# An attention-and-feed-forward kernel on one core: V products in fewer visits, maxima further ahead, and half of the rotary step on other engines

## The reference: what is computed

```
h = layernorm(x) * (1 + ca) + sa
q, k, v = split(h @ qkv_w.T + qkv_b); q, k = rope(q), rope(k)
attn = softmax(causal_mask(q @ k.T / sqrt(8))); x = x + ga * (attn @ v @ proj_w.T + proj_b)
h = layernorm(x) * (1 + cb) + sb
y = square(relu(h @ W_fc.T)) @ W_proj.T; x = x + gb * mean_of_5_spikes(y)
```

## Time and profile before

| | |
|---|---|
| median of 3 runs | 489.86 us (484.31 to 490.41) |
| the profiled execution | 488.89 us, of it a span of 487.2 us |
| busy: PE, DVE, ACT, POOL | 87%, 65%, 53%, 25% of the span |
| granted clock of PE, mean | 0.916 |

### The profile page before, as it was taken

One profiled execution on the slowest core, in us unless ns is written; L12 is line 12 of the kernel. 1 busy time (PEld: TensorE's weight loads), 2 busy tenths in 40 slices (PEclk: granted clock), 3 DMA queues, 4 the chain that ended last, 5 costly groups with the idle time before them and its releaser, 6 DMA issues.

```text
span 487.2 us, 14412 instructions
## 1 busy us (share of the span) xinstructions
PE 425.2 (87%) x6007; PEld 253.6 (52%) x6007; DVE 317.8 (65%) x719; ACT 256.0 (53%) x445; POOL 123.7 (25%) x159
## 2 busy tenths in 40 slices
PE   3448999889999999999999999999999999988752
PEld 2214564455546565565556654656556656645422
DVE  2768776747873978478865687388837674720735
ACT  1111465456476555755685447656665476666220
POOL 7624020501342141404240323213240310130210
PEclk9865699669999989999999699999999899999958
DMA  6166514141313232233214241323133220010000
GB/s 198 51 170 191 149 40 112 57 122 49 106 51 102 69 108 63 70 100 111 71 56 121 60 101 53 103 63 105 50 96 78 74 81 5 26 30 20 23 0 22
DMA packets 26043, 38.45 MB, mean 79 GB/s; under 512 B 5794, under 2 KB 20714, under 8 KB 23690
## 3 DMA queue, kind: packets, MB, share of 16 engines
q1 hardware_dynamic: 25978, 37.53, 26.8%
HBM read 26.35 MB, written 8.65 MB: 72 GB/s over the span
## 4 chain that ended last, share of the span: by engine, by line
PE 67%; DVE 16%; issue 4%; POOL 4%; ACT 4%; DMA 4%; SPq 1%; POOLq 0%; ACTq 0%; DVEq 0%
PE s_bank L447 15%; PE o_bank L498 12%; PE t_bank L480 10%; PE d_bank L554 6%; PE d_bank L547 5%; DVE negmax L778 4%; PE a_bank L518 4%; PE s_bank L453 3%; PE t_bank L485 2%; DMA den<-o_raw 2%; PE a_bank L525 2%; PE a_bank L467 2%; PE d_bank L537 2%; DVE xn L794 2%; DVE rot_s L814 2%
## 5 line engine op out<-in xcount | busy, mean ns | idle before, releaser
L778 DVE TENSOR_REDUCE negmax<-s_bank 128x1 f32<-128x448 f32 (+7 forms) x368 | 194.3, 566 | 99.9 <-PE s_bank L453 98.5
L664 ACT ACTIVATE probs<-t_bank 128x512 f32<-128x512 f32 x288 | 167.0, 596 | 118.0 <-PE t_bank L485 114.4
L447 PE MATMUL s_bank<-kf,qf 72*64 72x448 bf16 (+7 forms) x1024 | 127.1, 315 | 10.8 <-DVE negmax L778 10.5
L480 PE MATMUL t_bank<-qf,kf 74*64 74x512 bf16 (+7 forms) x1024 | 115.6, 297 | 4.2 <-ACT probs L664 4.1
L447 PEld LDWEIGHTS s_bank<-kf,qf 72*64 72x64 bf16 x1024 | 49.6, 114 | 101.8 <-DVE negmax L778 62.4
L498 PE MATMUL o_bank<-probs,v 128*32 128x512 f32 (+7 forms) x1024 | 92.5, 436 | 0.0
L453 PE MATMUL s_bank<-causal,identb 128*64 128x64 bf16 x1024 | 74.9, 202 | 0.0
L485 PE MATMUL t_bank<-causal_t,identb 128*64 128x64 bf16 x1024 | 65.2, 197 | 0.0
L480 PEld LDWEIGHTS t_bank<-qf,kf 74*64 74x64 bf16 x1024 | 41.4, 114 | 27.7 <-ACT probs L664 10.3
L485 PEld LDWEIGHTS t_bank<-causal_t,identb 128*64 128x64 bf16 x1024 | 49.1, 114 | 10.8
L453 PEld LDWEIGHTS s_bank<-causal,identb 128*64 128x64 bf16 x1024 | 49.4, 117 | 0.2
(11 more groups left out here) (106 smaller groups left out, 386.7 us busy)
## 6 DMA issues: line engine op xcount, KB each, us to landing
qf<-q_scr SPq DMA_DIRECT2D x15, 576.0 KB
kf<-k_scr SPq DMA_DIRECT2D x45, 192.0 KB
q_scr<-parts SPq DMA_DIRECT2D x24, 128.0 KB, 1.7
k_scr<-parts SPq DMA_DIRECT2D x24, 128.0 KB, 1.7
xa<-in_x SPq DMA_DIRECT2D x8, 256.0 KB, 3.5
o_t<-o_raw SPq DMA_DIRECT2D x60, 32.0 KB, 2.0
rden<-r_scr SPq DMA_DIRECT2D x15, 128.0 KB
out_y<-count SPq DMA_DIRECT2D x7, 256.0 KB, 2.3
```

The lines of the kernel that those rows point to most:

```text
L447: nc.tensor.matmul(bank[C * a:C * (a + 1), col:col + keys], qf[0:FR, slot, 2 * p + a, C * i:C * (i + 1)], kf[0:FR, slot, 2 * p + a, 0:keys ...
L480: nc.tensor.matmul(bank[C * a:C * (a + 1), col:col + w], kf[0:KX, slot, 2 * p + a, C * kb:C * (kb + 1)], qf[0:KX, slot, 2 * p + a, C * kb: ...
L664: nc.scalar.activation(probs[:, v, :], t_bank[u % 2][:, :], ACT.Exp, scale=SCALE).then_inc(e_done, 1)
L778: last = nc.vector.tensor_reduce(own[:, i, p:p + len(same)], cols, AX.X, ALU.max, negate=True)
```

## The change

Four things change. (1) The V products of a half run in four visits: key blocks 0, 1 and 7 after slot 9, 2 and 6 after slot 13, 3 and 5 after slot 0 of the next half, and 4 after its slot 1. Before they ran in eight, after slots 5, 9, 10, 13, 14, 17, 0 and 1. (2) `S_LEAD` is 31. (3) From batch 1 on, the two sine instructions of DVE are gone. ACT copies the projection with its bias to the other 64 partitions in two instructions (`swap_halves`, into the one buffer `rot_s[:, 0]`), POOL multiplies by the sines (`sines`, into `rot_s[:, 1]`), and DVE keeps the product with the cosines (`cosines`), which waits for ACT's copies as well. ACT's copies stand ahead of the exponentials of slots at = 25 and 29, DVE's product in slots at = 26 and 30, and POOL's product right ahead of each `rotary_sum`. (4) ACT's casts of the parts move a slot later, to after the exponentials of slots at = 29, 31, 33 and 35. SP's program stays as it is.

```diff
-S_LEAD = 29
+S_LEAD = 31
...
-PV_AFTER = {5: (0,), 9: (1,), 10: (7,), 13: (2,), 14: (6,), 17: (3,)}
-PV_LATE = {0: (5,), 1: (4,)}
+PV_AFTER = {9: (0, 1, 7), 13: (2, 6)}
+PV_LATE = {0: (3, 5), 1: (4,)}
...
-            for kb in (5, 4):
+            for kb in (3, 5, 4):
                 probs_times_v(HALVES - 1, kb)
...
+            def swap_halves(b, qk):
+
+                act.wait_ge(a_ready, 4 * b + QK + qk + 1)
+                reach(act, sines_done, 2 * (b - 1) + qk)
+                act.wait_ge(whole_done, 1)
+                for to, of in ((slice(0, 64), slice(64, P)), (slice(64, P), slice(0, 64))):
+                    nc.scalar.activation(rot_s[to, 0, :], a_bank[of, :], ACT.Identity, bias=bqk_sb[of, qk:qk + 1],
+                                         scale=1.0).then_inc(swapped, 1)
+
...
+            swap_halves(1, 0)
             for j in range(2):
                 take_part(1, 0, j)
+            swap_halves(1, 1)
...
-            TAKE_AT = {-8: (0, 0), -6: (0, 1), -4: (1, 0), -2: (1, 1)}
+            SWAP_AT = {-11: 0, -7: 1}
+            TAKE_AT = {-7: (0, 0), -5: (0, 1), -3: (1, 0), -1: (1, 1)}
...
+                if at - PER_BATCH in SWAP_AT and b + 2 < NB:
+                    swap_halves(b + 2, SWAP_AT[at - PER_BATCH])
...
+            def cosines(b, qk):
+                dve.wait_ge(a_ready, 4 * b + QK + qk + 1)
+                reach(dve, whole_done, 2 * (b - 1) + qk + 1)
+
+                dve.wait_ge(swapped, 2 * (2 * (b - 1) + qk + 1))
+                nc.vector.scalar_tensor_tensor(rot_c[:, qk, :], a_bank[:, :], bqk_sb[:, qk:qk + 1], cos_sb[:, :],
+                                               ALU.add, ALU.mult).then_inc(a_free, 1)
+
...
-            ROTARY_AT = {-11: (0, 0), -10: (0, 1), -9: (0, 2), -7: (1, 0), -6: (1, 1), -5: (1, 2)}
+            COSINES_AT = {-10: 0, -6: 1}
...
+            def sines(b, qk):
+
+                pool.wait_ge(swapped, 2 * (2 * (b - 1) + qk + 1))
+                pool.wait_ge(whole_done, 2 * b + qk)
+                nc.gpsimd.tensor_tensor(rot_s[:, 1, :], rot_s[:, 0, :], sin_sb[:, :], ALU.mult)\
+                    .then_inc(sines_done, 1)
+
...
             for qk in range(2):
+                sines(1, qk)
                 rotary_sum(1, qk)
...
                 if b + 2 < NB:
+                    sines(b + 2, 0)
                     rotary_sum(b + 2, 0)
                     left(b + 2, 0, 1)
                     left(b + 2, 0, 2)
+                    sines(b + 2, 1)
                     rotary_sum(b + 2, 1)
```

More of the change, by code:

```diff
@@ L245, in adaln_kernel @@
         rotated = sem("rotated")
+        swapped = sem("swapped")
+        sines_done = sem("sines_done")
         whole_done = sem("whole_done")
@@ L813, in rotary @@
                                       (slice(64, P), slice(0, 64), rot_s, sin_sb))[step]
-                nc.vector.scalar_tensor_tensor(dst[to, qk, :], bank[of, :], bqk_sb[of, qk:qk + 1], table[of, :],
+                nc.vector.scalar_tensor_tensor(dst[to, qk, :], bank[of, :], bqk_sb[of, qk:qk + 1], table[to, :],
                                                ALU.add, ALU.mult).then_inc(rotated if step < 2 else a_free, 1)
@@ L926, in _ @@
             gates()
-            for step in range(3):
-                rotary(1, 0, step)
+            cosines(1, 0)
             for k in range(7):
                 maxima(k)
-            for step in range(3):
-                rotary(1, 1, step)
+            cosines(1, 1)
             for k in range(7, scores_ahead(-1)):
                 maxima(k)
-            ROTARY_AT = {-11: (0, 0), -10: (0, 1), -9: (0, 2), -7: (1, 0), -6: (1, 1), -5: (1, 2)}
+            COSINES_AT = {-10: 0, -6: 1}
             SPIKES_AT = {41: 0, 42: 1, 43: 2, 44: 3, 45: 4}
@@ L945, in _ @@
                         normalise1(b + 2)
-                    if at - PER_BATCH in ROTARY_AT:
-                        rotary(b + 2, *ROTARY_AT[at - PER_BATCH])
+                    if at - PER_BATCH in COSINES_AT:
+                        cosines(b + 2, COSINES_AT[at - PER_BATCH])
                 if at == NU + 7:
@@ L1041, in deviation2 @@
                 inverse_deviation(b, mv2, ve2, rs2, var2_done, eps2_done, rs2_done)
+            def sines(b, qk):
[3 more added lines that the diff above has]
+                    .then_inc(sines_done, 1)
             def rotary_sum(b, qk):
                 pool.wait_ge(a_free, 3 * b + QK + qk + 1)
-                nc.gpsimd.tensor_tensor(whole[:, qk, :], rot_c[:, qk, :], rot_s[:, qk, :], ALU.add)\
-                    .then_inc(whole_done, 1)
+                reach(pool, sines_done, 2 * (b - 1) + qk + 1)
+                nc.gpsimd.tensor_tensor(whole[:, qk, :], rot_c[:, qk, :], rot_s[:, qk if b == 0 else 1, :],
+                                        ALU.add).then_inc(whole_done, 1)
             def left(b, qk, j):
@@ L1113, in _ @@
             deviation1(1)
+            pool.wait_ge(rotary_loaded, 16 * 2)
             for qk in range(2):
+                sines(1, qk)
                 rotary_sum(1, qk)
@@ L1193 @@
         "cosn": c(np.cos(angles).astype(np.float32)),
-        "sinn": c((np.sin(angles) * signs).astype(np.float32)),
+        "sinn": c(np.roll((np.sin(angles) * signs).astype(np.float32), 64, 0)),
         "place": c(np.stack([source, source_sum], 1)),
```

## The result

The changed kernel takes 531.95 us (median of 4 runs, 527.47 to 538.57), the kernel before 490.13 us (median of 4, 484.31 to 497.32). The ratio is 1.0859, with a 95% interval of 1.0788 to 1.093. Every ratio here compares only those executions of both kernels that ran in the faster of two states of the chip, so it need not be the quotient of the medians. The profiled execution took 527.47 us, of it a span of 525.7 us. That is 38.5 us more than the span of the profiled execution before.

What follows compares the result with a forecast made beforehand. PE was taken to set the pace, by what it issues and waits for. From 488.9 us, late waits (+20.2), batch 0 (+0.5), last batches (-2.0) and prologue (-0.5) gave 507.1, with the clock 519.6; forecast 520, range 498 to 533.

Steps and rivals of the forecast that it cites:

- The line to the transpose: Keys' projection to maxima's transpose, batches 1 to 5: PE's wait grows from 1.1 to 4.2 us, transpose 2.9 us later.
- The late start of the half: Next half's first scores, batches 1 to 5: a second wait of 2.2 us for the maxima's DMA, start 4.4 us late.
- a sign of being right: Once a batch PE would wait 1.5 to 3 us for the maxima's DMA.
- The clock: Granted clock falls in PE's waits of batches 1 to 5: 2.5 us a batch, between 0 and 5, +12.5 in all.
- The sign that I had named: The prediction would be wrong if the mean clock was not under 0.916.
- The visits: Fewer PE visits to V products save 0.21 us each, in and out together; 63 fewer in the program.
- part 1: Prediction's section on fewer V product visits: 10.8 us by changes of width, four visits a batch counted at 0.85 us.
- The lead: Two more units ahead cost about 0.5 us each before the first slot, nearly saved later; -0.5 us with DVE's relief.
- The last two batches: Batches 6 and 7 have no late way to the transpose and keep their saved visits: -2.0 us.
- The sum: Whole program: 488.9 + 20.2 + 0.5 - 2.0 - 0.5 = 507.1 us, 519.6 with the lower clock, stated as 520.
- Faster if ACT's cast ends early enough: Rival: queries' last cast on ACT ends by some 244.1 us, transpose finds its split ready; 478 to 479 us, chance 0.09.

Runs made afterwards that it cites:

- the filler run: Changed kernel, with the queries' projection computed four times more ahead of PE's wait at the maxima's transpose in batches 0 to 5; 520.14 us, ratio 1.0656.
- the run with the early split: Changed kernel, with POOL splitting the maxima right behind the queries' first subtraction, SP's order unchanged; 506.04 us, ratio 1.0373.

## Why the prediction was right, and where it was off

- **Direction and mechanism: right, and shown.** The rotary step and the casts alone give the whole loss. Mending the orders link by link takes it away again, and each mended link moved the wait to the next engine. That ACT would be the third I found only in the run.
- **The line to the transpose: right to 0.3 us.** Predicted 9.8 us behind the projection, measured 10.04. The copies took 1.39 us (I took 1.37, between 1.18 and 1.58), the cast ended at P+5.64 (5.6), the wait was 4.4 (4.2). The rest is POOL's sum, which starts 1.41 us after the product with the sines, not 1.2. The program has it wait for that one's result, while the product, whose inputs are ready, starts 1.11 us after the subtraction in front.
- **The late start of the half: right, but mostly not as a wait.** Predicted P+15.8, measured P+16.4 to P+17.2, and P+15.9 in the filler run, where the clock is up. A wait of 1.5 to 3 us for the maxima's DMA once a batch, which I had named as a sign of being right, did not come: PE idled for it in two of the five batches, 0.3 and 0.8 us. The lower clock stretched PE's way from the transpose on and so filled the wait. The filler run shows it in the open, 1.8 us, and the run with the early split 3.3.
- **The clock: it fell in all five batches, as predicted, for a little less.** I took 2.5 us a batch on top of both waits, 12.5 in all. It comes to about 9 us, an estimate from the filler run and the traces, very unequal: some 0.6 us in three batches, over 3 in two. The sign that I had named was a poor one, and by its letter it spoke against me: the mean clock of the changed kernel's execution is 0.916, not under the 0.916 of before. The execution before had its lower clock early, 0.80 up to the end of batch 0's projection where the changed one has 1.00, and that shows little in the time up to there (88.9 and 88.4 us). Behind that point the means are 0.94 and 0.90.
- **The visits: mis-sized.** I took 0.85 us a batch in part 1 and 0.4 more beside the waits. Alone they gave 0.3. The price of one visit was right. Three products before, apart, and the same three in one visit after (x24, a row that names only its first shape):

```profile
213.09 1.06 PE L498 MATMUL o_bank<-probs,v 128*32 128x512 f32 x8
216.99 0.96 PE L498 MATMUL o_bank<-probs,v 128*32 128x448 f32 x8
218.63 0.32 PE L498 MATMUL o_bank<-probs,v 128*32 128x64 f32 x8
...
230.99 1.93 PE L500 MATMUL o_bank<-probs,v 128*32 128x512 f32 x24
```

  That is 2.34 us for 1.93, 0.41 for two visits, as forecast. The step that failed is going from there to a batch, with six of eight visits at full price. PE's busy time fell by 0.8 us, not 1.3, and 0.5 of that turned into idling. Why it fell by so much less is not shown. The 10.8 us for the whole program came to some 5 (1% of 489).
- **The lead: the step that failed was taking it as neutral but for two units.** I did not ask what the first unit of a half waits for. It waits for the keys' features, and two slots sooner that DMA is not always there: 3.1 us in the changed kernel. And the lead costs 0.3 us in each undisturbed batch, alone and with the visits, which is all that the visits gain there.
- **The last two batches: wrong sign.** I took -2.0; from the last late start to the end it was +7.1. About 14 us more at the lower clock can account for it, 4.8 of them left over from batch 5's wait. The wait of 1.87 us for the features lies in the same stretch. Why the clock fell more often there is open.
- **The sum.** Forecast +30 us, measured +42, inside the range by 1 us only. In the profiled executions it is 38.5 against 30.7. For P to S and the clock I had 5 x 4.4 + 12.5 + 0.5 = 35, and 28.7 came, with the part of the clock that fell there. For all the rest I had -4.3, and +9.8 came. So the waits and the clock together were put 6 us too high, and the saved visits, the lead and above all the end of the program 14 us too low. That the two errors partly cancel, and the time falls inside the range, is luck.
- **Reading the rivals.** "Faster if ACT's cast ends early enough" was not the full condition. With the transpose's wait gone the loss was still 3.7%, since SP held the DMA, and with that mended still 2.5%, in part since ACT waited. One late result, the keys' sum, had three in-order engines behind it.

## What to carry to other kernels

On engines that run a fixed order, a job moved off a busy engine must be placed by what stands behind it, not by the load of the engine that takes it: POOL was busy for a quarter of the span, and still one product of 1.27 us in front of a short job that PE waits for came through whole (1.41 us from its start to the sum's). Walk the line from the moved job to the engine that sets the pace, through every cast, store and DMA issue in its program order, and then ask which wait is next once the first is gone. A lead that brings work forward also brings forward the time at which its inputs must have landed.

## What the runs showed of the hardware that I had not expected

- A lower clock can be nearly free. In the batch at 209.8 to 216.6 us it ended before the next half started, where PE waited for a DMA, and that half came 0.6 us later than in the filler run. In the batch at 267.8 to 281.5 it came 1.3 us later, and 4.3 us of its matmuls ran at half speed as well. Behind one and the same wait of 2.1 us it fell in four batches of five, and behind 3.0 us in three of five.
- Doing useless matmuls in a wait made the program faster: 3.7 us of them in each of six batches, and 2% off the ratio. The Trainium skill, TensorE: Matmul & The Clock Gate, Part 1, has activity lift the throttle; the trace agrees in four of the five batches, with a granted clock of 1.00 in the window shown against 0.53. In batch 1 the clock fell in the wait that was left.
- Two ACT copies from 64 partitions to the other 64 took 1.39 us together, 0.71 apart from start to start, against 0.51 for the 128-partition instructions that followed one another behind them (261.62 to 262.13).
